# Query copies between the two steps of a third tick, and a scatter issued two ticks earlier, in an attention and mixture-of-experts kernel

## The reference

```
h = rmsnorm(xn) * scale
q, k, v = h @ wq, h @ wk, h @ wv            # 16 heads of 64
w = softmax(q * 64**-0.5 @ k^T)             # over 512 keys, per head
attn = (w @ v) @ w_out + b_out

logits = silu(xn @ rw1 + rb1) @ rw2 + rb2   # 8 experts, top 2
for e in range(8):                          # softmax over the two chosen
    ffn += weight_e * (silu(xn @ w1[e] + b1[e]) @ w2[e] + b2[e])
out = x + attn + ffn
```

## Time and profile before

| | |
|---|---|
| median of 3 runs | 1963.85 us (1962.18 to 1966.85) |
| profiled execution, its time | 1968.87 us |
| its span | 1966.9 us |
| TensorE busy | 1851.2 us, 94% |
| VectorE busy | 1624.1 us, 83% |
| ScalarE busy | 1230.8 us, 63% |
| GpSimd busy | 707.0 us, 36% |

### The profile page before, as it was taken

One profiled execution on the slowest core, in us unless ns is written; L12 is line 12 of the kernel. 1 busy time (PEld: TensorE's weight loads), 2 busy tenths in 40 slices (PEclk: granted clock), 3 DMA queues, 4 the chain that ended last, 5 costly groups with the idle time before them and its releaser, 6 DMA issues.

```text
span 1966.9 us, 72822 instructions
## 1 busy us (share of the span) xinstructions
PE 1851.2 (94%) x31718; PEld 1113.1 (57%) x31718; DVE 1624.1 (83%) x2274; ACT 1230.8 (63%) x3009; POOL 707.0 (36%) x624
## 2 busy tenths in 40 slices
PE   8999999999999999998799999999999999999996
PEld 5555555555555555555455555555555555555554
DVE  6999999999999999989677777787868787777774
ACT  5666576656666666665466665757666666666662
POOL 3254554434453444441023223323323332333152
PEclk9999999999999999999899999999999999999999
DMA  3033331111111111110424334333333343333242
GB/s 92 21 79 109 105 88 45 41 43 41 40 44 37 46 46 46 41 40 26 115 67 83 72 67 83 73 78 72 84 67 71 85 83 71 74 68 63 66 72 49
DMA packets 148863, 127.48 MB, mean 65 GB/s; under 512 B 27040, under 2 KB 133408, under 8 KB 148512
## 3 DMA queue, kind: packets, MB, share of 16 engines
q1 hardware_dynamic: 117952, 102.10, 19.1%
q0 software_dynamic: 30592, 20.73, 8.0%
HBM read 90.59 MB, written 34.27 MB: 63 GB/s over the span
## 4 chain that ended last, share of the span: by engine, by line
PE 35%; DVE 24%; ACT 24%; issue 12%; DMA 3%; SPq 1%; POOL 1%; POOLq 0%; DVEq 0%; ACTq 0%
ACT PR L925 15%; DVE NM L568 10%; PE pair L330 8%; PE pair L469 7%; PE pair L311 7%; DVE PT L576 6%; DVE OT L585 3%; PE pair L343 3%; ACT ZZ L1012 3%; PE pair L296 3%; ACT ZT L1009 3%; DMA RB<-l_rows 2%; DVE HH L828 1%; PE pair L284 1%; PE pair L240 1%
## 5 line engine op out<-in xcount | busy, mean ns | idle before, releaser
L925 ACT ACTIVATE PR<-pair,NM 128x512 f32<-128x512 f32 x1024 | 690.5, 686 | 586.1 <-DVE NM L568 583.7
L576 DVE STREAM_TRANSPOSE PT<-PR 128x1024 f32<-128x1024 f32 x512 | 629.2, 1238 | 56.3 <-ACT PR L925 37.8
L568 DVE TENSOR_REDUCE NM<-pair 128x2 f32<-128x1024 f32 x512 | 599.4, 1211 | 32.1 <-PE pair L311 31.6
L311 PE MATMUL pair<-KS,QS 64*32 64x512 f32 x8192 | 503.1, 597 | 13.7 <-ACT PR L925 7.2
L330 PE MATMUL pair<-PT,V 32*64 32x256 f32 x16384 | 481.5, 378 | 15.8 <-ACT ZZ L1012 6.3
L1177 POOL DMA_INDIRECT out<-YS,IDW x156 | 245.7, 1575 | 658.1 <-DVE YS L835 472.7
L330 PEld LDWEIGHTS pair<-PT,V 32*64 32x64 f32 x16384 | 385.2, 131 | 164.4 <-issue 120.1
L311 PEld LDWEIGHTS pair<-KS,QS 64*32 64x32 f32 x8192 | 127.2, 106 | 238.1 <-issue 171.8
L828 DVE SCALAR_TENSOR_TENSOR HH<-ZT,ZZ 128x512 f32<-128x512 f32 x156 | 104.7, 691 | 172.0 <-ACT ZT L1009 89.6
L925 ACT ACTIVATION_READ_ACCUMULATOR PR<-pair,NM 128x1 f32 x1024 | 208.1, 203 | 0.0
L1124 POOL TENSOR_TENSOR TH<-TH,HS 128x512 f32<-128x512 f32 x64 | 81.6, 1276 | 244.3 <-ACT HS L965 244.3
(11 more groups left out here) (130 smaller groups left out, 1745.9 us busy)
## 6 DMA issues: line engine op xcount, KB each, us to landing
RB<-l_rows SPq DMA_DIRECT2D x128, 256.0 KB, 4.3
E<-w_tab SPq DMA_DIRECT2D x39, 512.0 KB, 4.5
XG<-slots SPq DMA_DIRECT2D x39, 264.0 KB, 4.1
E<-in_w SPq DMA_DIRECT2D x39, 256.0 KB, 3.8
xin<-in_x SPq DMA_DIRECT2D x16, 256.0 KB, 2.9
XQ<-in_x SPq DMA_DIRECT2D x16, 256.0 KB, 3.2
l_rows<-RT SPq DMA_DIRECT2D x256, 2.0 KB, 1.4
w_tab<-SPL SPq DMA_DIRECT2D x8, 512.0 KB, 2.8
```

The source lines that it names most:

```text
L311: m = pe.do.matmul(bank[2 * (s % 2) + r][32 * c:32 * c + 32, :], QS[rows, u % 2, c, at:at + 32], KS[rows, g % 2, c, :], start=True, stop=T ...
L568: dve.do.tensor_reduce(NM[:, step % 4], pairs[s % 2][:], AX.X, ALU.max, negate=True).then_inc(sem["dve_max"])
L576: dve.do.transpose(PT[:].rearrange("p c k q -> p (c k) q")[:, :, 32 * slot:32 * slot + 32], PR[:, step % PRB].rearrange("p r k -> p (r k)" ...
L925: act.do.activation(PR[:, step % PRB, r, :], bank[2 * (s % 2) + r], ACT.Exp, bias=NM[:, step % 4, r:r + 1], accum_out=RS[:, g % 2, r, at:a ...
```

## The change

ScalarE issued the two copies of the next unit's queries behind the exponentials of both steps of a third tick. It now issues them between the exponentials of the first and of the second step. GpSimd issued the scatter of the last routed block in tick 134, each DMA held until VectorE had done the first maximum of that tick. It now issues it in tick 132, with no such gate (a start of 0 leaves that wait out). Nothing is added or removed otherwise.

```diff
@@ scalar: attending(G)
-                if k == 2 and u + 1 < UNITS:
-                    queries(u + 1, 0)
-                    queries(u + 1, 1)
@@ scalar: loop over G
                 if u < UNITS:
                     probs(u, 2 * k)
+                    if k == 2 and u + 1 < UNITS:
+                        queries(u + 1, 0)
+                        queries(u + 1, 1)
                     probs(u, 2 * k + 1)
@@ gpsimd: route(G)
                 r, h = divmod(G, 8)
-                if r == NB and h == 6:
-                    scatter(r - 1, slice(0, 8), [2 * G + 1] * 8)
+                if r == NB and h == 4:
+                    scatter(r - 1, slice(0, 8), [0] * 8)
```

## The result

The changed kernel takes 1971.02 us (median of 11 runs, 1968.15 to 1974.48), the kernel before 1964.72 us on the same chip (median of 11, 1961.01 to 1968.11). The ratio is 1.0033, 95% interval 1.0024 to 1.0042: slower by 6.3 us, by more than 0.2%. A second measurement of the pair gave 1969.67 against 1964.85, a ratio of 1.0025 (1.0014 to 1.0036).

What follows compares the result with a forecast made beforehand. In the routing half no engine bounds alone: VectorE and ScalarE pace ticks 7 to 10 and 15 to 2, TensorE between. Routing +33.4, expert -10.9 and scatter -13.5 sum to +9.0: about 1973 us, range 1953 to 1982.

Steps and rivals of the forecast that it cites:

- The query copies' banks give nothing in the routing half: Routing half: banks freed 1.33 us earlier gain nothing, since TensorE's L223 then needs the later K copies; costed at 0.
- The pattern of held additions: Tick 2: GpSimd's products hold two of VectorE's four L709 additions and copy L712; NM 4.23 us after the first product.
- The rival in which one more addition slips through: Ticks 2 and 10: with a lead of 0.19 or more, NM is 2.99 after the product; total 1956 us; chance 0.20.
- 2.5 per tick 2: Tick 2 of seven blocks: NM 2.84 us later, less 0.3 of slack, makes 2.5 each, 17.5 together.
- The 0.3 of slack: Tick 2, routing half: TensorE's idle time ahead of the first K copy, taken off NM's 2.84 us delay.
- The 1.45 us that the prediction set beside the pair's 1.09: ScalarE's two query copies: the skill page's estimated duration, moving NM by some 0.2 us only; not used in the sum.
- Tick 10 and ticks 6 and 14: Routing half: held additions in tick 10 of eight blocks cost 10.4 us; later transposes in ticks 6 and 14 cost 5.5.
- Routing half, +33.4: Sum for the routing half's ticks 2, 10, 6 and 14: +33.4 us, bounds +5.5 and up to +45.
- Part 2, -13.5: Scatter moved from tick 134 to 132: removes TensorE's 12.34 us stall near 941 us and slow matmuls; bounds -15 and -11.
- the margin of 4: Last scatter: SyncE's chain of pads, fetch and store ends near 926, 4 us ahead of row RT.
- Expert half, -10.9: Expert half: L469 starts at once; residue X limits L223, so 18 waits cut at 0.5 us; bounds -3 and -13.4.
- The clock: Routing half rival: TensorE's clock also falls in about half of ten ticks with new waits; +7, 1980 us; chance 0.12.

Runs made afterwards that it cites:

- the one whose products wait for the counts: The changed kernel with GpSimd's first router product of a tick 2 or 10 held until L712 is done: 2079.91 us against 2111.63 for the kernel before.
- With the gate: The kernel before with only the scatter moved to tick 132, each DMA still held until that tick's first maximum: 1953.95 us, ratio 0.9948.
- the scatter alone: The kernel before with only the scatter moved to tick 132, ungated: 2104.82 us against 2111.63; on another chip 1951.06 against 1965.47.
- the kernel with the counts ahead: The changed kernel with VectorE's L709 additions and L712 copy ahead of the step's transposes: 2067.95 us against 2111.63 before; on another chip 1914.39 against 1965.47.

## Why the prediction was right, and where it was not

The forecast was 1973 in a range of 1953 to 1982, with 0.63 for slower; the time is 1971.02. Taken against the profiled execution the forecast was +9.0; the two profiled executions differ by +2.7 (1971.6 and 1968.87), the medians by +6.3.

- **The query copies' banks give nothing in the routing half** (cost 0). Right in the changed kernel, and for the reason given: L223 now waits for the K copies instead. The waits of 100 to 900 us have `L223 <- KS` at 12.9 us in 12 places where they had 3.2 in 5. TensorE's wait for L709's result is there as well, 23.5 us in 14 places (1.7 each, under L415, put down to issue; in the tick above L415 starts 0.10 behind L709's end), where it had 1.4 in two:

```profile
PE pair L415 <- issue: 23.5, 14, 2.5
...
PE pair L223 <- ACT KS L901: 12.9, 12, 1.1
```

- **The pattern of held additions** (one passes, held, passes in the gap, held, the copy held). Right. L709 came at q+2.28 (predicted q+2.27), the product at q+2.38 (q+2.39), NM at q+6.51 (predicted q+6.62). The rival in which one more addition slips through stood on a lead of 0.19; the lead was 0.10. The Trainium skill, GPSIMD Engine Reference, section 8, has the mechanism (shared SBUF interfaces, contention with VectorE's instructions of two SBUF inputs or in a two-port mode). The traces agree, and the changed kernel against the one whose products wait for the counts (on the other chip) isolates its price: 2.75 against 0.73 for the four additions, 1.19 against 0.17 for the copy. VectorE's instructions and their order are the same in both.
- **2.5 per tick 2.** Slightly low. The 0.3 of slack, which I took off for TensorE's idle time ahead of the K copies, wasn't recouped: the whole 2.73 persisted. 18.9 against 17.5. The 1.45 us that the prediction set beside the pair's 1.09 didn't bear on this kernel: the Trainium skill, ScalarE: Activation LUTs, Rules for kernel authors, gives its 0.3 us for an ACTIVATE whose bias is a pointer operand, and the query copies are given no bias; one of them takes 0.60.
- **Tick 10 and ticks 6 and 14.** 10.4 against 10.4 and 5.4 against 5.5. The medians, though, put ticks 6 and 14 nearer 9 (8.9, from two chips).
- **Routing half, +33.4.** Measured +37.8 at tick 134 in the trace, 36.8 by medians. Besides the 1.4 of tick 2 there is 1.0 in tick 130, which I had left out (its copies move as well), and the 2.4 of L687, which one execution has.
- **Part 2, -13.5.** Measured -13.6 in the trace, -14.4 by medians. The stall is gone. The reason was right, an intermediate size was not: SyncE's chain ended at 966.65, 1.2 us ahead of RT (ready at 967.87), not 4.

The middle stretch in the changed kernel's timeline, counterpart of the earlier trace rows:

```profile
939.65 0.14 DVE L743 COPY junk<-junk 1x1 f32<-1x1 f32 x1
940.07 1.00 POOL L1135 DMA_INDIRECT slots<-XR,IDX  x1 [23.60 <-DVE junk L743]
...
955.05 3.87 SPq L1298 DMA_DIRECT2D slots<-PAD  x4
...
964.92 1.73 SPq L1298 DMA_DIRECT2D slots<-PAD  x2
...
967.90 1.74 SPq L1239 DMA_DIRECT2D l_rows<-RT  x4
...
979.19 1.25 DVE L585 TENSOR_TENSOR OT<-pair,RB 128x512 f32<-128x512 f32 x2
```

The scatter starts 0.42 behind its marker, where it started 18.86 behind it. From its start to the first pad it took 14.98 us, where the earlier trace rows has 12.24: these 2.7 us are what the margin of 4 lost. With the gate, which starts the scatter 5.8 us later (910.03 against 904.23), the margin is overdrawn.

- **Expert half, -10.9.** This is the term that was mis-sized: -20.8 in the trace, -17.6 by medians, beyond its bound of -13.4. I cut each gain at 0.5, because L223 began at q+3.85 and X would end at q+3.25. The changed kernel's timeline of an expert tick:

```profile
1534.20 1.08 ACT L907 ACTIVATE QS<-pair 128x512 f32<-128x512 f32 x2
...
1535.31 0.60 PE L240 MATMUL pair<-idn,XG 128*128 128x128 f32 x4
...
1535.74 3.60 PE L469 MATMUL pair<-HH,E 128*128 128x512 f32 x8
...
1538.13 0.68 DVE L821 TENSOR_TENSOR X<-pair,X 128x512 fp32r<-128x512 f32 x1
...
1538.78 0.80 PE L223 MATMUL pair<-X,E 128*128 128x512 f32 x1
```

X is where it was predicted (q+2.60, its end q+3.28), and L469 starts 0.53 earlier. But L223 doesn't wait for X. Its recorded start, q+3.25, is 0.56 ahead of the recorded end of the L469 matmuls in front of it (1539.34). So it was in the earlier trace rows (1527.61 against 1524.50+3.67=1528.17), and its first matmul takes 0.80 in both traces. I read q+3.85 as the time from which X could bind; L469 ran until q+4.41 there, and X at q+3.28 is well ahead of that. In all 28 ticks L223 starts 3.04 behind L469's start after the change, and 3.11 (once 3.04) before. So the cut at 0.5 had no ground: two ticks with a counted wait of 0.97 gained 1.2. In 23 of the 28 the gain is 0.2 to 0.4 above the counted wait, and the five with no counted wait gained 0.2 to 0.7. The timelines show where the most of that lies: L469 takes 3.60 instead of 3.67, and where nothing holds it, it starts 0.17 ahead of L240's recorded end (1535.74 against 1535.31+0.60), while the idle time of the earlier trace rows is counted only from that end. Their 13.4 was thus no upper bound: 13.4 and 28 times 0.24 make 20.1, an estimate, near the 20.8.
- **The clock.** It fell as the rival said, but the price was wrong. In the kernel before it is at half once between 100 and 900 us (at 518.9), in the changed kernel twice (at 600.7 and 713.3, each behind a new wait of a tick 2), in its second trace five times. The steps of those ticks are no larger than the others. The mean granted clock is still 0.996 and 0.992 in the two traces after, against 0.992 before, since the 13.7 us at half from 945.6 on, at the stall, are gone. The rival's 7 us didn't come.

The two misses have opposite signs, +4.4 in the routing half and -9.9 in the expert half, and -0.1 in part 2; they bring the forecast's +9.0 to the trace's +3.4. So the time came out nearer to the forecast than the terms deserved. The sign rests on the routing half, where the mechanism held in every step.

What stays open: why L687 was caught in one execution, though it began 0.64 ahead of the first of the products that held it, and the 3.5 us by which ticks 6 and 14 seem dearer by medians than by the shifts.

## What to carry to other kernels

A copy moved ahead of other work on its engine is paid for by whoever needs that work; here 0.95 us on ScalarE moved four tiny additions and a copy of VectorE into the reach of GpSimd's products, and 0.9 us of work took 3.9. Look for what the delayed instruction will stand beside, down to tenths of a microsecond, and move the small operations to where the other engine is idle: that turned +4.8 us into -51.1. Slack in front of a matmul is read from the end of the matmuls ahead of it, not from its own recorded start. Where an edit gains in one stage and loses in another, condition it on the stage.

## What the runs showed of the hardware

- GpSimd's product of 128x512 (1.28 us) holds each VectorE addition of two SBUF operands (0.17 us alone) until it is over, even one of 8 columns; one gets through in the gap between two products. A copy of 8 columns from SBUF to SBUF is held in the same way (1.19 us). The scatters (0.96 us each) alone stretched nothing that I saw; L687 above began beside one, but its end is that of a product.
- The same kernel takes 1965 us in three of the measurements and 2111.63 in the other, on another chip. There TensorE's matmuls come one or two at a time, waiting for their issue, for about 8 us out of every 62 us of the routing half (16 times in the trace of the scatter alone). The mean granted clock is 0.971 there; after such a stretch it is at half (0.50 from 187.5 to 193.5 us). On the other chips the same 128 matmuls run through, as in the changed kernel's timeline:

```profile
1004.27 3.71 PE L330 MATMUL pair<-PT,V 32*64 32x256 f32 x128
```

No run here tells the cause. Where a kernel ran on both kinds of chip the sign was the same, the size was not (-6.8 and -14.4 us for the scatter, -43.7 and -51.1 for the kernel with the counts ahead).
